# A fused causal attention and ternary feed-forward kernel: start and end of the work written out job by job, with the second batch's deviations inside the first unit

## What is computed

```python
x = x + attn(layernorm(x), W_Q, W_K, W_V, W_O)   # causal softmax(q k^T / sqrt(128)) v, heads summed through W_O
x = x + (layernorm(x) * gamma + beta) @ ternary(weight).T + bias
```

## Time and profile before

| | |
|---|---|
| median of 3 runs | 897.38 us (896.47 to 899.69) |
| profiled execution, its own time | 896.73 us |
| its span, first to last instruction | 894.4 us |
| mean granted TensorE clock | 0.961 of full |
| busy: TensorE, VectorE, GpSimd, ScalarE | 820.2, 673.1, 548.8, 544.9 us |
| ACT_TABLE_LOAD instructions | 3 (start, first exponential, second layer normalisation) |

### The profile page before, as it was taken

The page is one execution under the profiler, slowest core; times in us unless marked ns, Lnnn a source line. Parts: engine busy times, 40 slices in busy tenths (PEclk is TensorE's granted clock), DMA queues, the critical chain, the costliest instruction groups (busy, mean ns, idle before and its releaser), DMA issues.

```text
span 894.4 us, 14482 instructions
## 1 busy us (share of the span) xinstructions
PE 820.2 (92%) x4790; PEld 731.5 (82%) x4790; DVE 673.1 (75%) x1448; ACT 544.9 (61%) x986; POOL 548.8 (61%) x283
## 2 busy tenths in 40 slices
PE   3879999999999999999999999999999999985264
PEld 3768889899988888888898998888888899974254
DVE  7577787877787787787877787787788777875444
ACT  1456666766666766666766766666667766654300
POOL 5026866677656855696577855684677666644521
PEclk7999999999999999999999999999999999998676
DMA  5045565566556565566555656556456655565011
GB/s 170 1 115 133 131 165 129 134 144 168 132 133 144 141 152 129 121 143 162 132 132 142 168 137 142 124 137 161 115 127 146 143 133 132 133 139 121 21 48 47
DMA packets 58696, 114.62 MB, mean 128 GB/s; under 512 B 17408, under 2 KB 21632, under 8 KB 58624
## 3 DMA queue, kind: packets, MB, share of 16 engines
q1 hardware_dynamic: 58624, 113.71, 53.2%
HBM read 10.88 MB, written 2.10 MB: 15 GB/s over the span
## 4 chain that ended last, share of the span: by engine, by line
PE 79%; DVE 7%; SPq 5%; DMA 3%; ACT 3%; issue 1%; POOL 1%; ACTq 0%; DVEq 0%
PE ring L460 21%; PE scores L498 20%; PE ring L439 17%; PE ring L448 9%; PE ring L469 9%; SPq L316 5%; DMA pT<-turn 3%; DVE norm L728 1%; PE ring L478 1%; DVE stats L710 1%; ACT turn L574 1%; POOL pT L383 1%; DVE scores L656 1%; PE ring L430 1%; ACT pT L594 1%
## 5 line engine op out<-in xcount | busy, mean ns | idle before, releaser
L383 POOL TENSOR_TENSOR pT<-pT 128x1024 fp32r<-128x1024 f32 x192 | 458.4, 2406 | 288.5 <-ACT pT L594 288.1
L656 DVE CUSTOM_DVE_ANT_0 scores<-scores,mask 128x128 f32<-128x128 f32 (+7 forms) x256 | 194.6, 760 | 157.3 <-PE scores L498 155.7
L574 ACT ACTIVATE turn<-scores,negmax 128x128 f32<-128x128 f32 (+7 forms) x256 | 189.4, 740 | 169.0 <-DMA pT<-turn 86.9
L498 PE MATMUL scores<-kT,qT 128*128 128x512 f32 (+3 forms) x1152 | 236.1, 344 | 11.7 <-ACT turn L574 10.1
L460 PE MATMUL ring<-pT,v 128*128 128x512 f32 (+3 forms) x1152 | 223.3, 348 | 9.4 <-POOL pT L383 9.4
L460 PEld LDWEIGHTS ring<-pT,v 128*128 128x128 f32 x1152 | 196.9, 190 | 39.1 <-issue 9.6
L594 ACT ACTIVATE pT<-pT 128x1024 fp32r<-128x1024 f32 x192 | 201.8, 1058 | 24.0 <-DMA pT<-turn 23.0
L498 PEld LDWEIGHTS scores<-kT,qT 128*128 128x128 f32 x1152 | 187.3, 190 | 34.1 <-ACT turn L574 14.1
L664 DVE STREAM_TRANSPOSE turn<-turn 128x128 f32<-128x128 f32 (+7 forms) x256 | 193.9, 768 | 2.3 <-ACT turn L574 2.2
L469 PE MATMUL ring<-wo_s,zT 128*128 128x256 f32 x768 | 114.7, 286 | 0.0
L439 PE MATMUL ring<-xT,wk_s 128*128 128x512 f32 x384 | 102.9, 404 | 8.9 <-DVE xT L752 7.8
(11 more groups left out here) (62 smaller groups left out, 462.7 us busy)
## 6 DMA issues: line engine op xcount, KB each, us to landing
pT<-turn SPq DMA_DIRECT2D x512, 128.0 KB, 2.3
pT<-turn SPq DMA_DIRECT2D x512, 64.0 KB, 2.0
acc<-in_x SPq DMA_DIRECT2D x4, 512.0 KB, 5.8
wq_raw<-in_wq SPq DMA_DIRECT2D x8, 256.0 KB, 3.6
wk_raw<-in_wk SPq DMA_DIRECT2D x8, 256.0 KB, 3.0
wv_raw<-in_wv SPq DMA_DIRECT2D x8, 256.0 KB, 3.1
norm<-in_wo SPq DMA_DIRECT2D x8, 256.0 KB, 2.9
out<-acc SPq DMA_DIRECT2D x8, 256.0 KB, 2.1
```

Source lines behind the costliest of these rows:

```text
L383: pool.tensor_tensor(chunk(half, LO, c), f32(chunk(half, LO, c)), f32(chunk(half, HI, c)), ALU.subtract).then_inc(plo_ready, 1)
L498: mm = pe.matmul(scores[:, t % 2, first + c:first + c + n], qT[:, par, a, t * P:(t + 1) * P], kT[:, par, m, c:c + n], start=(i == 0), stop ...
L574: act.activation(turn[half][:, :, 0:t + 1, q, :].rearrange("p b j i -> p j b i"), scores[:, t % 2, score_columns(t)].rearrange("p (j b i) ...
L656: dve.tensor_tensor_reduce(out=tile, in0=tile, in1=mask[:, S - (t + 1) * P:S], scale=-1.0, scalar=FAR, op0=ALU.add, op1=ALU.min, accum_out ...
```

## The change

The five tables of the steady part are kept as they are. They are now repeated only for units 2 to 30; what comes before and after is written out as one list for each engine (`START_TENSOR`, `END_TENSOR`, and so on), so that order and placement of every item there are new:

```diff
+STEADY_FROM = 2
+START_TENSOR = (
+    ("x", 0), ("x", 1), ("qk", 2, 0), ("qk", 0, 0), ("x", 2), ("x", 3), ("qk", 2, 1), ("s", 0, 0), ("s", 1, 0),
+    ("qk", 3, 0), ("qk", 1, 0), ("s", 2, 0), ("qk", 0, 1), ("s", 3, 0), ("qk", 3, 1), ("s", 4, 0), ("s", 5, 0),
+    ("x", 4), ("qk", 1, 1), ("s", 6, 0), ("s", 7, 0), ("v", 1, 0), ("v", 0, 0), ("s", 0, 1), ("x", 5), ("v", 0, -1),
+    ("s", 1, 1), ("v", 1, -1), ("x", 6), ("v", 1, 1), ("s", 2, 1), ("x", 7), ("s", 3, 1), ("v", 0, 1), ("qk", 2, 2),
...
+START_SCALAR = (
+    ("std", 0), ("std", 1), ("norm", 0), ("norm", 1), ("x", 0), ("x", 1), ("std", 2), ("norm", 2), ("norm", 3),
+    ("qk", 2, 0), ("qk", 0, 0), ("x", 2), ("x", 3), ("qk", 2, 1), ("exp", 0, 0), ("exp", 1, 0), ("qk", 3, 0),
+    ("qk", 1, 0), ("std", 4), ("exp", 2, 0), ("exp", 3, 0), ("norm", 4), ("qk", 0, 1), ("qk", 3, 1), ("exp", 4, 0),
...
+END_TENSOR = (
+    ("pv", 1, 29), ("qk", 1, 31), ("o", 1, 29), ("s", 0, 31), ("o", 3, 29), ("wsum",), ("s", 1, 31), ("o", 0, 29),
+    ("s", 2, 31), ("o", 2, 29), ("tp", 0), ("s", 3, 31), ("s", 4, 31), ("pv", 0, 30), ("tp", 1), ("tp", 2),
+    ("s", 5, 31), ("o", 1, 30), ("o", 0, 30), ("pvl", 0), ("s", 6, 31), ("tp", 3), ("tp", 4), ("tp", 5), ("s", 7, 31),
+    ("o", 1, 31), ("pv", 1, 30), ("o", 0, 31), ("tp", 6), ("xf", 0), ("o", 2, 30), ("pvl", 1), ("tp", 7),
+    ("o", 3, 30), ("tp", 8), ("tp", 9), ("o", 2, 31), ("xf", 1), ("xf", 2), ("pvl", 2), ("bw",), ("xf", 3),
+    ("o", 3, 31), ("ff", 0), ("xf", 4), ("ff", 1), ("ff", 2), ("xf", 5), ("ff", 3), ("xf", 6), ("ff", 4), ("xf", 7),
+    ("ff", 5), ("ff", 6), ("ff", 7),
+)
+END_SCALAR = (
...
+    ("exp", 5, 31), ("hip", 1, 3, 30), ("pvl", 0), ("tp", 3), ("tp", 4), ("tp", 5), ("std2", 0), ("exp", 6, 31),
+    ("exp", 7, 31), ("pv", 1, 30), ("tp", 6), ("xf", 0), ("table",), ("std2", 4), ("pvl", 1), ("tp", 7), ("tp", 8),
...
+END_GPSIMD = (
+    ("norm2", 0), ("norm2", 1), ("tern",), ("norm2", 2), ("norm2", 3), ("bias", 0), ("bias", 1), ("bias", 2),
+    ("bias", 3), ("bias", 4), ("bias", 5), ("bias", 6), ("bias", 7),
+)
```

```diff
+            def normalise(item):
+                kind, c = item
+                act.wait_ge(ln_step, ln_no[rstd_of("rstd2" if kind == "norm2" else "rstd", c)])
+                wait_norm_place(act, item)
+                for t in (2 * c, 2 * c + 1):
+                    last = act.activation(norm[:, t % 4, :], acc[:, t, :], ACT.Identity, bias=shift[:, t:t + 1],
+                                          scale=rstd[:, t:t + 1])
+                last.then_inc(norm_by_scalar, 1)
...
+            def turn_probs(k, dst):
+
+                at = 0
+                for t, j0, n in TURNS[k]:
+                    pe.wait_ge(probs_ready, LAST * QT + t + 1)
+                    for j in range(j0, j0 + n):
+                        mm = pe.transpose(dst[:, at * P:(at + 1) * P], last_turn(t)[:, j * P:(j + 1) * P], ident[:, :])
+                        at += 1
+                return mm
...
                 elif which == "o" and p == 0:
-                    sp.wait_ge(job_done, job["x", 12, 4, KD - 1] + 1)
+                    sp.wait_ge(job_done, job["x", NT // 2 - 2] + 1)
                     load(wo_raw, wo[0], wo_in)
```

More of the change, by code:

```diff
@@ L108, in exists @@
         if kind == "v":
-            return u >= -1 and v_job(item[1], u)[2] < PAIRS
+            return v_job(item[1], u)[2] < PAIRS
         if kind == "split":
[L111 to L122, removed]
+            return u % KINDS == (2 if item[1] == "v" else 3) and u < LAST - 1
@@ L123, in stream, with run_of @@
+        return kind != "load"
+    def run_of(start, table, end):
+        yield from start
+        for u in range(STEADY_FROM, LAST):
             for entry in table:
                 item = entry[:-1] + (u + entry[-1],)
-                if exists(item) and item not in done:
+                if exists(item):
                     yield item
-    HEAD = (("x", 0, 4, 0), ("x", 0, 4, 1), ("qk", 2, 0), ("qk", 0, 0), ("x", 4, 4, 0), ("x", 4, 4, 1), ("qk", 3, 0), ("qk", 1, 0))
-    steady = [i for i in stream(TENSOR, HEAD) if i[0] in JOBS_OF]
@@ L131, in attention_ffn @@
[L131 to L148, removed]
@@ L296, in chunk, with wait_norm_place @@
+        def wait_norm_place(engine, item):
+            kind, c = item
+            if c >= 2:
+                engine.wait_ge(job_done, job["x" if kind == "norm" else "xf", c - 2] + 1)
+            elif kind == "norm2" and c == 0:
+                engine.wait_ge(wo_ready, PAIRS)
         def chunk(half, part, c):
@@ L641, in _ @@
-            beside(len(steady))
+                elif kind in ("norm", "norm2"):
+                    normalise(item)
+                elif kind in ("std", "std2"):
+                    deviation(item)
+                elif kind == "table":
+                    act.activation(unused, eps[:, 0:1], ACT.Sqrt, bias=eps[:, 0:1])
+                else:
+                    act.wait_ge(job_done, job[item] + 1)
+                    for hi, _, src, scale in split_target(item):
+                        ins = act.activation(hi, src, ACT.Copy, scale=1.0 if scale is None else scale)
+                    ins.then_inc(jhi_ready, 1)
@@ L737, in run @@
+            for item in vector_run:
+                kind = item[0]
+                if kind == "max":
                     max_tile(*item[1:])
```

544 lines of the change are left out of this document (317 added, 227 removed), and 10 rows, old and new, of tables (END_SCALAR, END_VECTOR, START_TENSOR).

## The result

The changed kernel takes 826.04 us (median of 4 runs, 824.31 to 827.79) against 897.4: a ratio of 0.9201, 95% interval 0.9175 to 0.9227, so 71.4 us less. 832 was forecast, with a range of 822 to 850.

The account below looks back on a forecast made before the run. TensorE bounds the steady 708.5 us; the two ends, 186 us, are chains of waits. Span 894.4 - 16 (start) - 49 (end) = 829.4, with 2.3 around it 831.7, and 832 as the profiled execution lies 0.65 below the median; range 822 to 850.

Parts of the forecast that it names:

- The steady part carried over: Between the two marks, units 2 to 31: TensorE-bound, tables untouched, 24.34 us a unit, carried over as 708.5 us.
- The slower rival: Steady part: the new start sets a longer period, 2.5 us more a unit, total 904 us; chance 0.03.
- The end, 49 to 50 us shorter, TensorE and VectorE full: From the second mark: 60 us against 109.7, TensorE's work 52.8, VectorE about as much; 49 saved, bounds 38 and 52.
- The rival of a half-slow TensorE: End: short waits keep 11 us worth of work at 1.2 GHz, 38 saved, total 843 us; chance 0.15.
- The start, 16 us shorter: Up to the mark, TensorE's job qk(1, 2): from 76.2 to 60 us in three legs; bounds 8 and 20 saved.
- Two projections as slow as today (4.5 us in all): Start, leg to the first score tile: projections run from 10.4 to 15, first score tile at 18.7 against 25.4.
- The next leg: Start, first score tile to last flip of unit 0: VectorE fills up with 20.2 us, ending near 40.
- The wo load is an obstacle, waves at 43.5: Start, last leg: wo load waits for x job 6, waves start at 43.5 not 40, mark 16.4 later at 60.
- TensorE's own work, no bound: Start: TensorE's own work up to the mark is 42 us, so it does not bound the 60.
- The rival of a start that is a chain: Start: reload exposed and ScalarE normalisation delays projections, 8 saved instead of 16, total 840 us; chance 0.12.
- the rival with 14 more: Start and end: Identity outside the active table sets adds 14 loads, 18 us, total 848 us; chance 0.04.
- The moved deviation costed at 0: Start, between exponentials 1 and 2 of unit 0: two table loads and root, covered by VectorE's work; 2.9 us if uncovered.

Follow-up runs that it names:

- yardsticks: The changed kernel run twice more, unedited, beside groups of experiments: 824.53 us (ratio 0.9194) and 825.81 us (0.9205).
- an experiment brought back waits of 1.7 and 2.0: Changed kernel with all eight pairs at the start normalised by VectorE and not ScalarE: 831.38 us, ratio 0.9257.
- deviation earlier: Changed kernel with the deviation of pairs 4 to 7 before the first exponential and their statistics earlier, two table loads fewer: 826.75 us, ratio 0.9213.
- reload doubled: Changed kernel with one more empty square root, so two more table loads, ahead of exponential 4 of the first unit: 829.30 us, ratio 0.9227.
- fewer warm-up matmuls: Changed kernel with 32 warm-up matmuls in place of 48: 826.34 us, ratio 0.9214.
- first deviation behind the last exponential: Changed kernel with the end's first deviation taken behind exponential 7 in place of the empty root, two table loads fewer: 828.85 us, ratio 0.9222.
- one pair off GpSimd: Changed kernel with the end's normalisation of pair 1 moved from GpSimd to ScalarE, behind the last exponential: 823.18 us, ratio 0.9172.
- by DMA, first and second version: Changed kernel with the last unit through flips, waves, hip and lop again: 864.86 us; second, GpSimd freed for low parts, normalisations on ScalarE: 844.51 us.
- the later wo load: Changed kernel with the first wo load issued behind the first two quarters of unit 0's half 1 waves: 823.16 us, ratio 0.9176.
- The version with both fixes: Changed kernel with the later wo load and the end's normalisation of pair 1 on ScalarE together: 821.58 us, ratio 0.9155.

## Why the prediction was right, point by point

The result lies 6 us under the forecast: 3.3 of it in the start, 1.3 in the end, 0.8 in the steady part, and 0.6 because the profiled execution is not below the median this time. The range holds it, though its lower end was added up loosely: 20 and 52 us saved make 825 in the forecast's own sum and not 822.

*The steady part carried over.* Right: 707.7 against 708.5. The slower rival, a longer period that the new start would set, is out.

*The end, 49 to 50 us shorter, TensorE and VectorE full.* Right in size (59.4, predicted 60) and in kind: TensorE is busy for 53.07 of 59.41, and the sum of the prediction was 52.8. Up to +25 it had done 24.7 (predicted 24), and it ended at +56.0 (predicted +54), VectorE at +56.8 (+56). Exponential 7 ended at +29.0 (+30). Two of its steps were off. GpSimd's normalisation was put at 0.77 for 256 columns from the bias addition; it took 1.22, and in place of costing nothing it held TensorE for 1.75 us (in the yardsticks it came as late, behind a wait for VectorE). The last bias additions, named as what the last ff waits for, were no bound: eight of 1.29 us, 10.0 in all and not 12.3, over at +54.3. And "with something for waits" was then spent in part on the wait for the normalisation. The rival of a half-slow TensorE fell: the clock was 1.00.

*The start, 16 us shorter.* It was 19.3, and the difference is in terms that were mis-sized. "Two projections as slow as today (4.5 us in all)": they took 3.0 at a granted clock of 1.00, with 1.57 us of wait before them; where an experiment brought back waits of 1.7 and 2.0, the clock was 0.50 and the two took 4.8. With this and shorter ways between the x jobs the first score tile came at 15.9 and not 18.7. (The first transposes were at 8.0 and not 7.1, behind warm-up matmuls that the prediction has no term for; the run with 32 of them shows that this cost nothing.) The next leg was 19.3 us and not 21.3. "The wo load is an obstacle, waves at 43.5": it was, for 3.2 us, but at 38.0 since x job 6 was earlier; moving it gave 1.4. Then 13.35 and not 12.1 us to exponential 4, and 5.15 and not 4.3 from there to the mark, with the slow matmuls in it: 2.1 us of what the first two legs and the waves had gained were given back here. The leg to the last flip was called VectorE's; in the yardstick TensorE is fuller there (19.58 of 20 us from 20 to 40, VectorE 18.81, ScalarE 19.04), and the run with less work for the other two found it busy for 19.84. So "TensorE's own work, no bound" is right for the way to the mark as a whole but wrong for this leg. Normalisation on ScalarE was worth 5.5 us at the mark, 1.8 of them by the clock of two projections. The rival of a start that is a chain, with 8 us saved, is out.

*Seven table loads.* Right: the trace has seven, and none around an Identity, so the rival with 14 more is out.

*The moved deviation costed at 0.* Right, by the run without it: the first reload is free. The bound of 2.9, if the cover is gone, is about right too: the second one cost 2.2. At the end the prediction costed the reload at nothing but saw no gain in it; without it the end was 62.6 us and not 59.4 to 60.8. The Trainium skill says to do all of one table set before changing ("ScalarE: Activation LUTs", Rules for kernel authors). At the end of this kernel that order was the slower one. The Trainium skill also adds a drain of 1.4 us to each load ("ScalarE: Activation LUTs", What ACT_TABLE_LOAD costs). The trace doesn't agree: the activation before ends at 788.51, and load, root, load, exponential follow at 788.53, 789.83, 790.15 and 791.44.

## What to carry to other kernels

Read a program that is full in its middle by stretches: here 186 us at both ends held all but 0.8 of the 70.4 us, and adding up each engine's work for the end, with the last chain behind it, gave its length within a microsecond (the start, followed leg by leg, was 3 us off). A table reload costs ScalarE's time; what it costs the kernel was nothing at one place and 2.2 us two tiles later. Ask who waits for ScalarE at that place and who waits for the result, because a root taken earlier for two more loads can be worth it. Where one DMA load with a wait of its own stands ahead of a queue that others wait for, put it behind the part of the queue that is due.

## What was not expected of the hardware

The same wait of TensorE before the last score tiles of unit 1 was followed by the low clock in some profiles and by the full clock in others. These are the ten profiles in which it is over 1.7 us, with what the 12 matmuls behind it took:

| profile | wait, us | 12 matmuls, us |
|---|---|---|
| changed kernel | 2.22 | 4.39 |
| yardstick, first and second | 2.28, 2.24 | 2.89, 2.88 |
| deviation earlier | 2.32 | 4.44 |
| reload doubled | 1.75 | 4.32 |
| fewer warm-up matmuls | 2.35 | 2.89 |
| first deviation behind the last exponential | 1.81 | 4.19 |
| one pair off GpSimd | 2.36 | 4.06 |
| by DMA, first and second version | 2.19, 2.15 | 4.09, 2.88 |

The length of the wait doesn't decide it: behind 1.75 and 1.81 the 12 matmuls took over 4 us, behind 2.35 they took 2.89. On one chip all four profiles have the low clock there, on another all three have the full clock, and a third chip gave one of each; so chance and chip can't be told apart here. With waits of 0.8 and 0.6 (the later wo load, alone and with the other fix) the matmuls were fast in both profiles. The version with both fixes spread over 2.1 us and the changed kernel over 3.5, 2.6 and 3.4; that the first is the cause of the second was not tried alone.

A small instruction of VectorE (L886, two or four columns, two operands in SBUF) takes 0.16 us. When it starts while GpSimd is in an addition of two tensors, it ends when that addition does, within 0.06 us. In the first yardstick:

```profile
9.89 1.28 POOL L516 TENSOR_TENSOR wq_s<-wq_raw,wq_s 128x512 fp32r<-128x512 f32 x1
...
10.37 0.81 DVE L886 SCALAR_TENSOR_TENSOR std<-mv,rstd 128x4 f32<-128x4 f32 x1
```

GpSimd ends at 11.17 there, VectorE at 11.18. At the end of the same profile the instruction starts at 797.85, 0.02 us behind an addition of the ternary weight, and takes 1.25. In the changed kernel's profile both start at 799.97, and it takes 0.16. Beside GpSimd's tensor-scalar operations and its clearing of `turn1` it takes 0.16 too.

A tensor-scalar operation of 128x256 in float32 with two column operands takes GpSimd 1.22 us, almost what an addition of two tensors of twice the size takes it (1.29).
